# A scan kernel's dt and u rows: spread over partitions from SBUF instead of through DRAM, and two softplus sums moved from VectorE to TensorE

## The reference, cut to what matters

```python
xn = layernorm(x)                                   # x is [2, 1024, 512]
proj = xn @ W_in.T                                  # 1024 channels of x, 1024 of gate
x = silu(conv4(proj_x)); ssm = x @ W_x.T            # 32 columns for dt, 16 for B, 16 for C
ts, B, C = rms(ssm[..., :32]), rms(ssm[..., 32:48]), rms(ssm[..., 48:])
dt = softplus(ts @ W_dt.T + b_dt)                   # one number per token and channel
def step(state, (dt_t, B_t, C_t, u_t)):             # state is [1024 channels, 16]
    state = state * exp(dt_t[..., None] * A) + (dt_t * u_t)[..., None] * B_t
    return state, sum_n(state * C_t)
s = ((y + x * D) * silu(gate)) @ W_out.T
out = x_in + s * silu(top2_of_8_experts(xn))
```

## Time and profile before

| | |
|---|---|
| median of 3 runs | 1053.31 us (1052.16 to 1054.01) |
| the profiled execution | 1050.33 us, of which 1048.4 us are its span |
| granted TensorE clock, mean of the span | 0.914 |
| VectorE busy | 983.2 us (94%) |
| GpSimd busy | 904.9 us (86%) |
| TensorE busy | 853.0 us (81%) |
| ScalarE busy | 728.4 us (69%) |
| spread, `rep<-rep_rows`, from issue to landing of one of its DMAs | 6.2 us (median), 128 DMAs |
| store, `rep_rows<-dtu`, from issue to landing | 3.1 us (median), 32 DMAs |

### The profile page before, as it was taken

The page is one execution under the profiler, slowest core; times in us unless marked ns, Lnnn a source line. Parts: engine busy times, 40 slices in busy tenths (PEclk is TensorE's granted clock), DMA queues, the critical chain, the costliest instruction groups (busy, mean ns, idle before and its releaser), DMA issues.

```text
span 1048.4 us, 10364 instructions
## 1 busy us (share of the span) xinstructions
PE 853.0 (81%) x2756; PEld 317.2 (30%) x2756; DVE 983.2 (94%) x1027; ACT 728.4 (69%) x1281; POOL 904.9 (86%) x320
## 2 busy tenths in 40 slices
PE   8945458989878998999746859989888979988478
PEld 5321113333323343333211313333323323323123
DVE  6779999999999999999999899999999997999996
ACT  3656757888877767888664566888778775767543
POOL 0616899989989998998898988899988989999996
PEclk9986669999989999999976869999999998999778
DMA  9948559887779666675843753866548575664735
GB/s 335 350 154 311 203 200 354 294 298 272 264 271 336 226 226 243 240 276 203 282 116 144 212 209 121 309 236 233 203 178 308 204 255 191 237 237 171 283 54 144
DMA packets 86585, 245.93 MB, mean 235 GB/s; under 512 B 9344, under 2 KB 10752, under 8 KB 79872
## 3 DMA queue, kind: packets, MB, share of 16 engines
q1 hardware_dynamic: 67712, 197.03, 53.0%
q10 hardware_dynamic: 12672, 31.46, 7.6%
q0 software_dynamic: 6144, 16.78, 6.0%
HBM read 183.11 MB, written 62.13 MB: 234 GB/s over the span
## 4 chain that ended last, share of the span: by engine, by line
POOL 22%; DVE 21%; PE 20%; issue 12%; ACT 12%; DMA 10%; SPq 2%; ACTq 0%; DVEq 0%; POOLq 0%
POOL drive L605 13%; DVE sc_ps L1207 7%; DMA rep<-rep_rows 5%; POOL drive L618 4%; ACT sc_ps L818 4%; DVE drive L1207 4%; DVE drive L1217 4%; PE x_ps L1532 3%; PE dt_ps L1460 3%; DMA rep_rows<-dtu 3%; PE f_ps L1485 3%; PE y_ps L1500 2%; PE x_ps L1396 2%; POOL slot_x L569 2%; POOL moe L590 1%
## 5 line engine op out<-in xcount | busy, mean ns | idle before, releaser
L605 POOL TENSOR_TENSOR drive<-rep,b_all 128x2048 f32<-128x2048 f32 x127 | 579.6, 4603 | 37.6 <-DMA rep<-rep_rows 34.0
L818 ACT ACTIVATE sc_ps<-rep,a_neg 128x512 f32<-128x512 f32 x512 | 332.2, 681 | 101.8 <-DVE drive L1217 72.1
L1500 PE MATMUL y_ps<-drive,stack 128*32 128x512 f32 x1024 | 151.6, 668 | 104.1 <-DVE drive L1217 66.2
L618 POOL TENSOR_TENSOR drive<-drive,c_all 128x1024 f32<-128x1024 f32 x92 | 219.8, 2389 | 11.8 <-ACT state L797 9.7
L1207 DVE TENSOR_TENSOR_SCAN sc_ps<-sc_ps,state,drive 128x512 f32<-128x512 f32 x164 | 202.5, 1272 | 5.6 <-ACT sc_ps L818 3.9
L1207 DVE TENSOR_TENSOR_SCAN sc_ps<-sc_ps,drive 128x512 f32<-128x512 f32 x164 | 193.5, 1214 | 10.2 <-ACT sc_ps L818 6.1
L1217 DVE TENSOR_TENSOR drive<-sc_ps,c_all 128x1024 f32<-128x1024 f32 x164 | 199.2, 1215 | 2.8
L1485 PE MATMUL f_ps<-w_ring,xT_slot 128*128 128x512 f32 x368 | 173.0, 614 | 23.4 <-ACT xT_slot L828 22.9
L1460 PE MATMUL dt_ps<-xnT,w_g 128*128 128x512 f32 x232 | 125.1, 689 | 24.1 <-ACT dtu L785 24.1
L1207 DVE TENSOR_TENSOR_SCAN drive<-sc_ps,state,drive 128x512 f32<-128x512 f32 x92 | 113.7, 1267 | 6.6 <-ACT sc_ps L818 6.6
L1207 DVE TENSOR_TENSOR_SCAN drive<-sc_ps,drive 128x512 f32<-128x512 f32 x92 | 109.7, 1208 | 2.0 <-POOL drive L605 0.9
(11 more groups left out here) (189 smaller groups left out, 1048.8 us busy)
## 6 DMA issues: line engine op xcount, KB each, us to landing
rep<-rep_rows SPq DMA_DIRECT2D x128, 512.0 KB, 6.2
w_ring<-wring SPq DMA_DIRECT2D x46, 1024.0 KB, 6.3
rep_rows<-dtu ACTq DMA_DIRECT2D x32, 512.0 KB, 3.1
x_slot<-slot_x SPq DMA_DIRECT2D x46, 256.0 KB, 6.7
slot_rows<-y_slot ACTq DMA_DIRECT2D x46, 256.0 KB, 4.4
w_g<-wg_in SPq DMA_DIRECT2D x32, 256.0 KB, 7.1
w_x<-wx_in SPq DMA_DIRECT2D x24, 256.0 KB, 4.3
slot_x<-zeros SPq DMA_DIRECT2D x1, 5888.0 KB, 20.6
```

Of the source, the lines that this page charges most:

```text
L605: pool.tensor_tensor(drive[:, m % RING, :, :], rep[:, n % 2, :, 1, :], b_all[:, q:q + 1, :].broadcast_to([P, NR, TC]), ALU.mult).then_inc( ...
L618: pool.tensor_tensor(drive[:, m % RING, 0:2, :], drive[:, m % RING, 0:2, :], c_all[:, q:q + 1, :].broadcast_to([P, 2, TC]), ALU.mult).then ...
L818: act.activation(sc[:, r, :], rep[:, n % 2, r, 0, :], ACT.Exp, scale=a_neg[:, lo:lo + 1]).then_inc(decay_ok, 1)
L1500: last = pe.matmul(y_ps[CH * r:CH * (r + 1), :], stack[:, :], drive[:, m % RING, r, :], start=False, stop=(m % NQ == NQ - 1))
```

## The change

The DRAM tensor `rep_rows`, the DMA that fills it and the semaphore `s_dtu` go. SyncE issues the spread with `dtu` itself as its source, once `times_x` and `keep_dt` have signalled. Since `dtu` is now read by the spread, `times_x` and `keep_dt` of tile k wait until the spread of tile k - 1 has landed. In the first tile `times_x(1)` is moved behind `route_rows` for this. And the steps of tiles 17 and 21, which are made in tiles 15 (chunk 1, block 7) and 19 (chunk 2, block 3), leave `VECTOR_LOG` and `STEPS_AMONG_SCANS`: their sums are made on TensorE.

```diff
-VECTOR_LOG = (0, 1, 2, 3, 4, 5, 7, 8, 10, 11, 12, 16, 17, 18, 19, 21, 23, 24, 26, 27, 28, 29, 31)
+VECTOR_LOG = (0, 1, 2, 3, 4, 5, 7, 8, 10, 11, 12, 16, 18, 19, 23, 24, 26, 27, 28, 29, 31)
-STEPS_AMONG_SCANS = (1, 3, 5, 10, 15, 19, 21, 26, 27, 29)
+STEPS_AMONG_SCANS = (1, 3, 5, 10, 21, 26, 27, 29)
...
             def spread(k):
-                sp.wait_ge(s_dtu, 16 * (k + 1))
+                sp.wait_ge(dt_ok, k + 1)
+                sp.wait_ge(dt_cp, k + 1)
                 if k >= 2:
                     sp.wait_ge(decay_ok, UNITS * (k - 1))
                     drives_done(sp, NQ * (k - 1))
                 for r in range(NR):
-                    rows = rep_rows[k % 2, CH * r:CH * (r + 1), :].rearrange("c (o f) -> c o f", o=1)
+                    rows = dtu[CH * r:CH * (r + 1), :, :].rearrange("c k (o t) -> c o (k t)", o=1)
...
             def keep_dt(k):
                 act.wait_ge(dt_ok, k + 1)
                 if k:
-                    act.wait_ge(s_dtu, 16 * k)
+                    rep_landed(act, k - 1)
                 act.copy(dt, dt_ps[:, :]).then_inc(dt_cp, 1)
...
-            def keep_rows(k):
-                act.wait_ge(dt_cp, k + 1)
-                act.wait_ge(dt_ok, k + 1)
-                if k >= 2:
-                    rep_landed(act, k - 2)
-                act.dma_start(rep_rows[k % 2], dtu[:, :, :].rearrange("p k t -> p (k t)")).then_inc(s_dtu, 16)
...
                 dve.wait_ge(x_ok, k + 1)
                 if k:
-                    dve.wait_ge(s_dtu, 16 * k)
+                    rep_landed(dve, k - 1)
                 dve.tensor_tensor(u, dt_ps[:, :], xy[:, c % 2, t, :], ALU.mult).then_inc(dt_ok, 1)
...
-            step_sizes(1)
+            larger_part(1)
+            less_rounding(1)
+            plus_log(1)
             route_rows()
+            times_x(1)
```

More of the change, by code:

```diff
@@ L117, in scan_moe @@
 def scan_moe(nc, x, wx_in, wg_in, wdt_in, wxp, wring, gate_w, means, a_log, conv_w, conv_b, d_skip,
-             route_consts, bc_dram, rep_rows, xn_rows, xnT_rows, slot_x, slot_rows, s_rows, out):
+             route_consts, bc_dram, xn_rows, xnT_rows, slot_x, slot_rows, s_rows, out):
     with ExitStack() as ctx:
@@ L255, in scan_moe @@
         s_wdt = sem("s_wdt")
-        s_dtu = sem("s_dtu")
         s_wr = [sem(f"s_wr{s}") for s in range(2)]
@@ L916, in _ @@
             keep_dt(0)
-            keep_rows(0)
             softplus(1)
@@ L941, in _ @@
                 diagonal(n)
-                if t < NT - 1:
-                    keep_rows(n + 1)
                 store_slot(b, left_slot)
@@ L1685 @@
     bc = nc.dram_tensor("bc_rows", (NCH, 2 * N, TC), F32, kind="Internal").ap()
-    rep_rows = nc.dram_tensor("rep_rows", (2, P, 2 * TC), F32, kind="Internal").ap()
     xn_rows = nc.dram_tensor("xn_rows", (TOK, H), F32, kind="Internal").ap()
@@ L1692 @@
     out = nc.dram_tensor("out", (TOK, H), F32, kind="ExternalOutput").ap()
-    scan_moe(nc, *aps, bc, rep_rows, xn_rows, xnT_rows, slot_x, slot_rows, s_rows, out)
+    scan_moe(nc, *aps, bc, xn_rows, xnT_rows, slot_x, slot_rows, s_rows, out)
     r = run_bass_kernel_spmd(nc, [arrays], core_ids=[0])
```

## The result

| | before | after |
|---|---|---|
| median, same chip | 1052.91 us | 1107.95 us (1097.84 to 1114.62) |
| ratio | | 1.049 [1.0417, 1.0562] |
| profiled execution, its span | 1050.33, 1048.4 us | 1106.35, 1104.4 us |
| granted TensorE clock, mean | 0.914 | 0.899 |

The change makes the kernel 4.9% slower. One of the four runs of after (1114.62 us) was in a slower state and is left out of the ratio; the other three have a mean of 1104.6 us, 52 us above the 1053.0 of before, and the two profiled executions are 56 us apart. The forecast was 1052.2 us and the range ended at 1061 us. The slow rival had the right sign and too small a size.

A forecast was written before the change was run, and what follows sets the result against it. VectorE was taken to bound some stretches, GpSimd others. Terms +1.9 + 3.0 - 2.9 - 1.1 - 2.0 = -1.1 us took 1053.3 to 1052.2 us; range 1044.5 to 1061 us, leaving out 2 in 10.

The forecast's parts named there:

- slow rival: Reads of 32 partitions slow throughout, spread 4 to 5 us longer; at 5 us, +6.8 us, 1060 us; chance 0.23.
- Part 1, the trip through DRAM: Spread issued without the store: 2.8 us saved in tile 0, up to 8.8 where DMAs queued, nothing in tile 16.
- Part 2, X: Extra time of a whole four-DMA spread read from SBUF: taken as 3 us, bounds 0 and 5.1 us.
- Part 3, quiet tiles: Tiles without queued DMAs: 2.8 us saved against 3 us lost, GpSimd ahead of VectorE, so nothing.
- tile 1: GpSimd's start after the first spreads: later by twice the spread's extra time less 4.1 us; +1.9 us.
- tile 16: SyncE is not free earlier, so nothing saved; GpSimd's 3.23 us wait grows by the spread's extra time: +3.0 us.
- tile 26: Spread 4.1 us earlier, GpSimd's 2.94 us wait goes, VectorE's 4.04 us wait shrinks as much: -2.9 us.
- tile 28: Spread 1.4 us earlier, more than GpSimd's 1.09 us wait, where GpSimd decides: -1.1 us.
- Part 4, the two sums: Two softplus sums moved from VectorE to TensorE: -2.0 us in tile 19, nothing in tile 15.
- third rival: The sums on TensorE cost what they save: the -2.0 us go, 1054 us; no separate chance, within the forecast.
- Part 5, the new waits: `times_x` and `keep_dt` wait for the previous tile's spread: nothing, at most some tenths of a us in the first tile.
- TensorE waiting for weights: Sign, not in the sum: TensorE waiting for weights or slots would show the DMA engines had become the bound.

The follow-up runs named there:

- e10: e1 with four chained 512-byte transfers, each waited for, ahead of each spread; 1066.08 us, 1.0144 of before.
- e3: The kernel before with only the two sums moved to TensorE, spread still through DRAM; 1050.21 us, 0.9991 of before.
- e1: The changed kernel with each spread DMA reading every fourth partition instead of 32 neighbours, channels reordered to suit; 1041.4 us, 0.9909 of before.
- e9: e1 with two chained 512-byte transfers, each waited for, ahead of each spread; 1044.88 us, 0.995 of before.
- e13: e1 with six chained 512-byte transfers, each waited for, ahead of each spread; 1103.55 us, 1.0514 of before.

## Why the prediction was wrong

The kernel's own steps, in the order of the forecast:

- **Part 1, the trip through DRAM.** Right in mechanism, its size a little too large: from the copy to the first packet of the spread it was 4.9 us in before and 2.7 in after (medians), 2.2 us saved where I took 2.8.
- **Part 2, X. The first step that failed.** From its first packet to its landing a spread took 7.7 us before and 14.1 after: X = 6.4 us. I took 3 and called 5.1 the upper bound. The 1.45 came from a store of two packets per engine, over in 0.4 us; a spread keeps 16 engines at work for 32 packets each, and there the factor was 330 / 187 = 1.8. The bound of 5.1 us was a doubling of the engine time, which I took as 5.1 us from the store's packets of 0.16 us; the spread's own took 187 ns, 6.0 us in all, and that rose by 4.6 us. The landing of the last packet rose by more: the four issues take 7.8 us instead of 2.5. The slow rival's argument, that packets which overlap must be slower than their mean, was the right one.
- **Part 3, quiet tiles: nothing. The step that cost most.** Had I put X = 6.4 into my own terms, the sum would have been +8.7 (tile 1), +6.4 (tile 16), -0.7 (tile 26), +2.0 (tile 28) and -2.0: 14.4 us, 1068 us. The other 40 us or so arise in tiles for which the sum had no term. I reasoned that 2.8 saved stood against 3 and that GpSimd was ahead; both were judged at one tile. A spread is released by work that stands behind the drives of the spread before it, so its lateness comes back one tile later. A table of single waits, each priced where it stood in before, can't show that. I had left out nine of the 13 waits of before, because VectorE did not wait behind them; that GpSimd waited in so many tiles was the sign that the slack of the loop was nearly used up; e10 shows that 1.6 us more lateness than in before already cost 1.4%.
- **Part 3, the four places.** Tile 16: the wait grew by 5.0 us, as at X = 5. Tile 1: GpSimd's first drive came at 108.82 us instead of 101.66, 7.2 us later, where the term gives 8.7 at X = 6.4. Behind it VectorE waits 4.89 us at a scan where it waited 0.19 before, and the wait of 0.90 us that the forecast priced is still there with 0.91; the sign was right. Tile 26: its wait should have gone and is there with 2.87 us. The forecast's own test would say that the trip through DRAM did not make it late, but the test assumed X = 3: the spread was issued 0.1 us behind the copy instead of 7.1, and the longer transfer used that up (from the copy to the landing 17.0 us, before 17.4). Tile 28: 4.13 us instead of none.
- **Part 4, the two sums.** -2.0 us forecast, nothing told from zero in any of three surroundings, so the term stays open; it could never have decided the result. VectorE's busy time was to fall by 4 us; it fell by 2.6 in e3 and by 0.9 in after. In after `times_x` waits 15.4 us in six tiles for TensorE's sums, but the third rival (the sums cost what they save) is no explanation of the result: without the sums moved it is as slow (1.0497).
- **Part 5, the new waits.** Right for 30 of 31 waits of `times_x`. The one of tile 1 took 2.84 us where I had said some tenths, and as all of VectorE stands behind it, the copies of tiles 1 and 2 are 2.5 us late. e1 keeps these waits and is the fastest kernel.
- **TensorE waiting for weights** did not decide in after (3.0 us for w_x), but loads did take longer, w_g 9.6 us instead of 7.1.
- **The sums.** Two slips change nothing: at X = 3.3 the terms of the slow rival add up to -0.2 us and not zero, and the chances add up to 0.25 for same and 0.34 for slower, where 0.27 and 0.32 stand.

## What to carry to other kernels

In this kernel the copy over partitions from SBUF to SBUF was worth having only when every DMA read partitions from all over SBUF: try a layout of the channels in which it reads every fourth partition, not a block of 32. That made the loss of 4.9% a gain of 0.9%. Before a transfer is made later, look for the loop: what releases it, and does that stand behind its own consumer on any engine or queue? If so, price a delay per tile, not per wait; and measure the slack of such a loop directly, with small chained transfers ahead of it, before betting on it.

## What was not expected of the hardware

- Packets of 4 KB from SBUF took 159 ns or about two or four times as long, depending on which 32 partitions a DMA reads, with the same bytes and the same number of packets (159, 311, and a tenth over 652 ns).
- Issues of DMAs on SyncE took longer where the packets ahead were slow: up to 4.3 us for one issue of a spread in after, 0.93 in before, 1.8 in e1, with the same number of DMAs in the spread. The four issues of a spread took 7.8 us in the median tile, in which nothing else of that queue is issued.
- A chained transfer of 512 bytes, issue, landing and wait together, delays the queue by about 1.1 us in the first tile, where little else runs (the first spread of e10, behind four of them, was issued at 70.08 us, that of e1 at 65.53), and by 1.7 in the median tile (from the copy to the first packet 5.5 us in e9, 2.0 in e1, for two of them).
- The granted clock of TensorE, mean of the span, went with the lateness and not with the packets: 0.898 in e13, 0.899 in after, 0.914 in before, 0.921 in e1. A stretch has to be compared with the same work, though. This is after at the times of the earlier trace rows at a chunk's end:

```profile
554.00:600.00 46.00, 25.55 (x69) 6.68 (x70) 38.37 (x37) 23.95 (x37) 37.45 (x15) 0.59 0.46 102
```

0.59 lies between the two levels (0.5 is 1.2 GHz, 1.00 is 2.4 GHz); TensorE was busy 25.55 of the 46 us. The earlier trace rows has 0.80 here, but after runs some 30 us behind at this point. The kernel before had a clock of 0.71 from 522 to 568 us, with TensorE busy 21.68 us, and after has 0.80 from 586 to 632 us. So 0.80 to 0.71 is another piece of the work under the same window, and only 0.71 to 0.59 can be put down to the change.
